# Linear layer of a graph network: own rows added to x by GpSimd, bias added in PSUM by TensorE

## The reference

```python
out = segment_sum(Wh[src] * alpha[:, :, None], dst)   # edges and one self loop per node
x = x + out
x = x + einsum('bsi,oi->bso', layernorm(x), weight) + bias
```

## Time and profile before

| | |
|---|---|
| median of 3 runs | 7913.96 us (7913.86 to 7914.26) |
| profiled execution, its own time | 7921.19 us |
| its span | 7919.4 us, 115948 instructions |
| PE busy | 5157.7 us (65%) |
| DVE busy | 3609.7 us (46%) |
| ACT busy | 3195.4 us (40%) |
| POOL busy | 4682.5 us (59%) |
| mean granted TensorE clock | 0.743 |

### The profile page before, as it was taken

How to read it: one execution, slowest core, us unless ns; L and a number is a source line. 1 busy time by engine, 2 the same in 40 slices (tenths; PEclk the granted TensorE clock), 3 DMA queues, 4 the chain that set the end, 5 groups by cost and what they waited for, 6 DMA issues and landing times. The chain is left out here.

```text
span 7919.4 us, 115948 instructions
## 1 busy us (share of the span) xinstructions
PE 5157.7 (65%) x22196; PEld 4061.3 (51%) x22197; DVE 3609.7 (46%) x8810; ACT 3195.4 (40%) x8284; POOL 4682.5 (59%) x4875
## 2 busy tenths in 40 slices
PE   2689867777645555779734344566677566676796
PEld 2566544454434444579734344345456345455795
DVE  7634467777820000453500000466666566667533
ACT  2533244444343433333333333244444344444432
POOL 5032277777567777125277777677774777773253
PEclk9779977777777777779755555577778777777698
DMA  2432144444233333222311111344443344442324
GB/s 61 176 78 83 48 120 117 115 117 116 83 100 108 109 109 108 66 78 70 100 28 28 28 28 26 91 115 115 115 114 83 103 115 115 114 114 66 106 69 137
DMA packets 417887, 726.44 MB, mean 92 GB/s; under 512 B 129365, under 2 KB 278315, under 8 KB 414167
## 3 DMA queue, kind: packets, MB, share of 16 engines
q0 software_dynamic: 208256, 503.58, 23.6%
q1 hardware_dynamic: 202475, 208.74, 8.5%
q10 hardware_dynamic: 6508, 8.01, 0.3%
HBM read 596.63 MB, written 123.54 MB: 91 GB/s over the span
## 5 line engine op out<-in xcount | busy, mean ns | idle before, releaser
L1017 POOL DMA_INDIRECT g_rows<-table,src_idx x2326 | 2218.0, 954 | 710.0 <-issue 709.4
L1292 PE MATMUL g_p_win<-g_rows,g_hot 128*128 128x264 f32 (+1 forms) x4704 | 1502.2, 477 | 44.5 <-issue 41.4
L1292 PEld LDWEIGHTS g_p_win<-g_rows,g_hot 128*128 128x128 f32 x4704 | 1069.1, 238 | 305.3 <-issue 94.0
L1182 ACT ACTIVATE g_hot<-iota,near 128x128 f32<-128x128 f32 x2352 | 720.7, 386 | 411.7 <-PE g_p_win L1292 375.7
L1017 POOL DMA_INDIRECT g2p_rows<-rows,src_idx x771 | 736.3, 955 | 235.2 <-issue 235.2
L1017 POOL DMA_INDIRECT gcnp_rows<-table,src_idx x771 | 734.8, 953 | 235.5 <-issue 235.5
L1098 DVE TENSOR_TENSOR g_rows<-g_rows,g_p_w 128x1792 f32<-128x1792 f32 x336 | 679.0, 2021 | 27.0 <-ACT g_rows L1210 2.7
L1201 ACT ACTIVATE g_resets_f<-fwd_reset 128x112 f32 (+3 forms) x168 | 54.8, 326 | 1176.1 <-DVE g_b L1069 1061.3
L1249 PE MATMUL g_p_turn<-slide,g_a 128*8 128x128 f32 (+1 forms) x168 | 59.0, 351 | 715.6 <-DVE g_a L1057 715.6
L1105 DVE TENSOR_TENSOR agg<-agg,g2p_p_out 128x256 f32 x112 | 42.1, 417 | 943.3 <-PE g2p_p_out L1254 943.3
L1105 DVE TENSOR_TENSOR agg<-agg,gcnp_p_out 128x64 f32 x112 | 20.3, 221 | 957.0 <-PE gcnp_p_out L1254 957.0
(11 more groups left out here) (831 smaller groups left out, 10986.2 us busy)
## 6 DMA issues: line engine op xcount, KB each, us to landing
g_stage<-table SPq DMA_DIRECT2D x3328, 1.0 KB
g_rows<-table,src_idx POOLq DMA_INDIRECT x2326
g2p_stage<-rows SPq DMA_DIRECT2D x1664, 1.0 KB
gcnp_stage<-table SPq DMA_DIRECT2D x1664, 0.2 KB
back<-agg SPq DMA_DIRECT2D x7, 1792.0 KB, 34.9
rows<-r_row SPq DMA_DIRECT2D x98, 128.0 KB, 3.0
gcn_row_in<-back SPq DMA_DIRECT2D x14, 896.0 KB, 7.3
c_row<-back SPq DMA_DIRECT2D x14, 896.0 KB, 13.5
```

Of the source, the lines that this page charges most:

```text
L1017: gp.indirect_dma_start(rows[:, s, j, 0:width + H], None, table, bass.IndirectOffsetOnAxis(g.src_idx[:, at:at + 1], 0)).then_inc(got[s], 16)
L1182: last = nc.scalar.activation(hot[:, j, :], g.iota[:, :], ACT.Square, scale=-1.0, bias=g.near[:, bass.ds(c * J + j, 1)])
L1292: last = nc.tensor.matmul(p_win[:, 0:W], hot[:, j, :], rows[:, s, j, :], start=(j == 0), stop=(j == J - 1))
```

## The change

- GpSimd does each group's own rows alone: it multiplies them by `share` and then adds them to x, a whole group (128 x 1792) in one operation. `own_added` now comes from GpSimd. `mix` is gone from VectorE; its `add` waits for `scaled` and `own_added`.
- The bias is no longer added by GpSimd. `bias_row` is a matrix of zeros with the bias in its first row; before each tile's two products TensorE multiplies a matrix of ones with it into the same PSUM buffer. `take` no longer waits for `biased`.
- GpSimd clears `bias_row` first; SP waits for that (`blank`) before it loads the bias and the second group's own rows.

```diff
--- before.py
+++ after.py
@@ -606,7 +606,7 @@
                 behind(i)
         ahead_of_all(NT, normalise, copy)
 
-    def tensor(self, pe, rhs):
+    def tensor(self, pe, rhs, bias=None):
         nc = self.nc
 
         def turn(i, s):
@@ -621,8 +621,10 @@
             pe.wait_ge(self.copied, i + 1)
             if i >= 2:
                 pe.wait_ge(self.taken, i - 1)
+            if bias is not None:
+                nc.tensor.matmul(self.out[s][:, :], self.g.ones[:, :], bias, start=True, stop=False)
             for b in range(2):
-                last = nc.tensor.matmul(self.out[s][:, :], self.xt[:, s, b, :], rhs[:, b, :], start=(b == 0), stop=(b == 1))
+                last = nc.tensor.matmul(self.out[s][:, :], self.xt[:, s, b, :], rhs[:, b, :], start=(b == 0 and bias is None), stop=(b == 1))
             last.then_inc(self.multiplied, 1)
         ahead_of_all(NT, turn, multiply)
 
@@ -1340,13 +1342,13 @@
     with Phase(nc, name) as ph:
         own = ph.sb("own", [P, 2, GROUP, D])
         total, inv, share = (ph.sb(n, [P, NT, H]) for n in ("total", "inv", "share"))
-        w_in, wt, bias_wide = ph.sb("w_in", [P, 2, D]), ph.sb("wt", [P, 2, D]), ph.sb("bias_wide", [P, D])
+        w_in, wt, bias_row = ph.sb("w_in", [P, 2, D]), ph.sb("wt", [P, 2, D]), ph.sb("bias_row", [P, D])
         p_w = ph.ps("p_w", [P, 4, P])
         first, second = GroupNorms(nc, g, ph, "a"), GroupNorms(nc, g, ph, "b")
         prod = FedProducts(nc, g, ph, D, first)
         seq, w_loaded, bias_loaded, turned, placed = (ph.sem(n) for n in ("seq", "w_loaded", "bias_loaded", "w_turned", "w_placed"))
-        shared, own_scaled, own_added, scaled, added, biased, made, stored = (
-            ph.sem(n) for n in ("shared", "own_scaled", "own_added", "scaled", "added", "biased", "made", "stored"))
+        blank, shared, own_scaled, own_added, scaled, added, made, stored = (
+            ph.sem(n) for n in ("blank", "shared", "own_scaled", "own_added", "scaled", "added", "made", "stored"))
         loaded = [ph.sem(f"loaded{s}") for s in range(2)]
         heads_of = lambda t: t.rearrange("p a (h c) -> p a h c", h=H)
         wide = lambda t: t.unsqueeze(3).to_broadcast([P, GROUP, H, C])
@@ -1358,7 +1360,8 @@
                     sp.dma_start(own[:, n % 2, :, :], table[n * GROUP * P:(n + 1) * GROUP * P, 0:D].rearrange("(t p) d -> p t d", p=P)).then_inc(loaded[n % 2], 16)
                 load(0)
                 sp.dma_start(w_in[:, :, :], w.rearrange("(b p) n -> p b n", p=P)).then_inc(w_loaded, 16)
-                sp.dma_start(bias_wide[:, :], bias.rearrange("(o n) -> o n", o=1).to_broadcast([P, D])).then_inc(bias_loaded, 16)
+                sp.wait_ge(blank, 1)
+                sp.dma_start(bias_row[0:1, :], bias.rearrange("(o n) -> o n", o=1)).then_inc(bias_loaded, 16)
                 load(1)
                 for n in range(NG):
                     if n + 2 < NG:
@@ -1379,16 +1382,12 @@
                     o = own[:, n % 2, :, :]
                     gp.wait_ge(loaded[n % 2], 16 * (n // 2 + 1))
                     G.tensor_tensor(heads_of(o), heads_of(o), wide(share[:, of(n), :]), ALU.mult).then_inc(own_scaled, 1)
+                    gp.wait_ge(own_scaled, n + 1)
+                    G.tensor_tensor(g.x[:, of(n), :], g.x[:, of(n), :], o, ALU.add).then_inc(own_added, 1)
+                G.memset(bias_row[:, :], 0.0).then_inc(blank, 1)
                 gp.wait_ge(shared, 1)
-                own_share(0)
-                own_share(1)
-                gp.wait_ge(bias_loaded, 16)
                 for n in range(NG):
-                    if n + 2 < NG:
-                        own_share(n + 2)
-                    for t in range(n * GROUP, (n + 1) * GROUP):
-                        gp.wait_ge(prod.normal, t + 1)
-                        G.tensor_tensor(g.x[:, t, :], g.x[:, t, :], bias_wide[:, :], ALU.add).then_inc(biased, 1)
+                    own_share(n)
 
             @block.vector
             def _(dv):
@@ -1408,14 +1407,9 @@
                     sums = g.agg[:, of(n), 0:D]
                     V.tensor_tensor(heads_of(sums), heads_of(sums), wide(inv[:, of(n), :]), ALU.mult).then_inc(scaled, 1)
 
-                def mix(n):
-                    sums = g.agg[:, of(n), 0:D]
-                    dv.wait_ge(scaled, n + 1)
-                    dv.wait_ge(own_scaled, n + 1)
-                    V.tensor_tensor(sums, sums, own[:, n % 2, :, :], ALU.add).then_inc(own_added, 1)
-
                 def add(n):
                     x = g.x[:, of(n), :]
+                    dv.wait_ge(scaled, n + 1)
                     dv.wait_ge(own_added, n + 1)
                     V.tensor_tensor(x, x, g.agg[:, of(n), 0:D], ALU.add).then_inc(added, 1)
                     dv.wait_ge(added, n + 1)
@@ -1423,7 +1417,6 @@
                 def take(t):
                     x = g.x[:, t, :]
                     dv.wait_ge(prod.multiplied, t + 1)
-                    dv.wait_ge(biased, t + 1)
                     V.tensor_tensor(x, x, prod.out[t % 2][:, :], ALU.add).then_inc(prod.taken, 1)
                     if t >= 1:
                         again(t - 1)
@@ -1447,8 +1440,6 @@
                         if n + 1 < NG:
                             if u == 0 and n >= 0:
                                 scale(n + 1)
-                            if u == 1:
-                                mix(n + 1)
                             if u == 2:
                                 add(n + 1)
                             if u >= 3:
@@ -1491,7 +1482,8 @@
                     for ib in range(2):
                         nc.tensor.transpose(p_w[:, 2 * ob + ib, :], w_in[:, ob, ib * P:(ib + 1) * P], g.ident[:, :]).then_inc(turned, 1)
                 pe.wait_ge(placed, 4)
-                prod.tensor(pe, wt)
+                pe.wait_ge(bias_loaded, 16)
+                prod.tensor(pe, wt, bias_row[:, :])
 
 
 def tile_of(t, i, n):
```

## The result

The changed kernel has a median of 7930.18 us over 17 runs, the kernel before 7915.27 over 17. Sixteen of the 17 runs lie between 7924.13 and 7934.47; one took 8051.35 at a lower granted clock and is left out of the ratio. The ratio is 1.0017, with an interval from 1.0009 to 1.0025. Measured again beside the experiments the two have 7924.18 and 7912.19, a ratio of 1.0014 (1.0005 to 1.0024). So the change costs 12 to 15 us, which is just under the 0.2% that the forecast took as the bound. The forecast had 1.3 us the other way and a range that ended at 7923.

What follows compares the result with a forecast made beforehand. VectorE, with its two-input SBUF operations and GpSimd's excluding each other, was taken to bound the stage; 9.7 - 12.9 - 6.5 - 1.1 + 6.5 + 0 + 3 = -1.3 us from 7913.96 gave 7912.5, range 7899 to 7923.

Steps and rivals of the forecast that it cites:

- The dense block: Stage's first part: ten GpSimd own-row operations run back to back and hold VectorE's two-input operations off, +9.7 us net.
- turns: In the block, VectorE and GpSimd alternate, each waiting out the other's operation; one GpSimd turn more or fewer is 3.2 us.
- The late four: GpSimd's multiplications and additions of groups 5 and 6: each addition holds a chain of small VectorE operations, +6.5 us together.
- VectorE's seven additions: Own-row additions taken off VectorE: five outside the first window save 2.57 us each, -12.9 us; two counted with the block.
- what clears: After the block: L484 no longer waits in three groups, -6.5 us; VectorE's wait for a bias addition goes, -1.1 us.
- The product on TensorE: 49 products of ones with the bias matrix: 0 in the middle groups, +3 us in the last window.
- TensorE did not become the bound: Rival: in the five middle groups TensorE bounds at the low clock, up to +36 us, 7948; chance 0.05.
- The third: Rival: all fourteen GpSimd operations hold VectorE for their whole length, 44 us against 18; +15 us, 7929; chance 0.1.

Runs made afterwards that it cites:

- e4_price: Changed kernel with other GpSimd operands and operations in the last two groups: dense multiplication 3.98 and 3.95 us, addition with broadcast share 3.21 us.
- e5_short_add: Changed kernel with GpSimd adding the broadcast share to x in place of the scaled own rows: 7916.38 us, ratio 1.0004.
- e9_chain_free: Changed kernel with GpSimd's multiplication of group 2 also waiting for the first fit: 7919.27 us, ratio 1.0009.
- e6_no_product: Changed kernel without the 49 products of ones with the bias matrix, bias left out of the result: 7920.33 us, ratio 1.0010.
- e1_bias_only: Changed kernel with own rows multiplied by GpSimd but added by VectorE as before; TensorE still adds the bias: 7910.37 us, ratio 0.9999.

## Why the prediction was wrong

By its own sum, from VectorE's first operation to the last shift (148.3 before, 158.6 after, so +10.3 where -1.3 was forecast). Of the 11.6 us between them 7.5 lie in the first part and 4.4 in the five windows; the tail gives 0.3 back.

- **The dense block: +9.7 forecast, +17.2 measured.** This is the step that failed. Two causes, told apart by runs. The addition was priced at 3.1 to 3.2 us from the row of the multiplication, "since the undisturbed row has the same shape"; the shape was the same and the operand was not, and it takes 3.96 (e4_price). That is 3.7 us of the 7.5 (e5_short_add). The rest is turns: the forecast let two GpSimd operations, or three, into the chain behind the first statistics, and put the shift of group 0 at 28 to 31 us from the start (it says rstd, but the 2104.65 beside it is the end of the row of the shift); four got in behind the one that already ran, and it came at 37.2. With that chain free it comes at 24.5 and the first part is 8.4 us shorter, 6.3 with the window behind it (e9_chain_free), which also takes away the turns that the forecast had counted.
- **The late four: +6.5 forecast.** The windows with them are 19.8 and 19.7 against 14.8 without, +10 in all. The hold of L468 was foreseen at 3.1 each and is 3.6 and 3.5; that the product then comes later and at a lower granted clock, 1.4 us each, was not. These two windows have a clock of 0.83, where the forecast expected more than the 0.82 of before: behind the held L468 TensorE is idle for 5.08 and 4.99 us, and its products for the next tile take 1.91 us in place of 1.03.
- **VectorE's seven additions, and what clears: -12.9, -6.5, -1.1.** Right but for 1 us in all: the windows without GpSimd are 14.7 to 14.8, where the forecast had 14.3 and some waits. Together with the late four the five windows gave -9.6 where -14.0 stood.
- **The product on TensorE: 0 in the middle, +3 in the tail.** The tail, from 18.1 to 20.8 us up to the last shift, is right, and the product is the whole of it (without it the tail is 17.9, e6_no_product); but a turn of TensorE there grew from 1.25 to 1.51 us, not to the 1.7 of the forecast. In the middle it is 0.5 us a group as forecast where no GpSimd operation runs, and the granted clock rose to 0.98 and 1.00 there, also as forecast, without the products too. VectorE's waits for products in the five windows went from 4.2 to 7.7 us; 2.8 of that is counted above with the late four, and the 0.7 left is near the forecast's zero. Over the stage the product costs 5.2 us against a kernel without it. Against the bias additions on GpSimd it is the better of the two, by 4.1 us (e1_bias_only), since those also hold VectorE.
- **The rivals.** TensorE did not become the bound. The third, that GpSimd lets VectorE in less often, came nearest: it said +15 us for the stage's holds at worst, and the stage measured +10.3, the total +12 to +15. Its number is near partly by luck: the holds and the one wait for GpSimd's addition that I count in VectorE's rows, over an undisturbed 2.02 and 0.17 us, make 36 us in the changed kernel, not its 44, because not every operation held VectorE, though the additions are longer than its 3.15. It had 0.1, and the range left out its upper half. It deserved more: the forecast itself followed two orders of turns, took numbers at their favourable end, and knew a row in which a chained operation of seven elements was held for 3.17 us.
- **The page.** The forecast cited the Trainium skill, GPSIMD Engine Reference, section Elementwise — side-by-side cycle accounting, whose 2.6 cycles an element gave an estimate of 3.9 us, and set it aside for a row of 3.21. The rows after, 3.95 to 3.98 for dense operands, agree with the page; the row chosen was of another kind of operand. The page alone would not have mended the forecast, which came to 7921 by it: the turns were wrong all the same.

## What to carry to other kernels

When an operation moves to GpSimd, don't only ask whether GpSimd has the time: its two-input operations and VectorE's two-input operations from SBUF exclude each other, so the move saves VectorE 2.0 us and takes back up to 4.0 wherever the two meet. A chain of short dependent operations was what suffered most beside a block of GpSimd work, since GpSimd got in again after every one to three links; release GpSimd by a semaphore when VectorE starts a stretch of statistics or sums from PSUM (this turned +10 us into -13 with no other change). And take a price from a row only if its operands are of the same kind, broadcast or dense, not just of the same size.

## What the runs showed of the hardware

- A GpSimd tensor_tensor of 128 x 1792 in float32 takes 3.20 to 3.22 us when its second operand is broadcast over 32 columns, and 3.95 to 3.98 when both are dense, for addition and multiplication alike (e4_price). The broadcast form also has its operands split into heads.
- VectorE and GpSimd took turns when both had operations waiting. Operations of 1792 elements went one for one; of the operations of seven elements one to three got through before the next was held (L468 to L470 in e9_chain_free). Five links of a chain of operations of 0.17 us took 1.40, 3.17, 3.92, 3.13 and 3.19 us in the changed kernel.
- A tensor_scalar of VectorE with one tensor input in SBUF is held too: L471 took 3.84 us in e9_chain_free and ended with GpSimd's addition, and 3.84 and 3.83 in e6_no_product and e4_price. The Trainium skill, SBUF — State Buffer, section SBUF: two separate sides, says that one pair of ports is shared and locked for a whole instruction against VectorE's operations with two SBUF inputs or in a mode that uses both ports. The held rows with two inputs agree with it; those of L471 do if it ran in such a mode, which no row shows. The batch statistics kept their 0.40 to 0.43 us in every run, beside GpSimd's operations too.
